# Perceiver layer on one core: the last key's context product in one piece of 128 columns for four heads

## What is computed

```python
q = (query @ Wq).reshape(b, sq, NUM_HEADS, HEAD_DIM).transpose(0, 2, 1, 3)
k = (key @ Wk).reshape(b, sk, NUM_KV_HEADS, HEAD_DIM).transpose(0, 2, 1, 3)
v = (value @ Wv).reshape(b, sk, NUM_KV_HEADS, HEAD_DIM).transpose(0, 2, 1, 3)
...
scores = jnp.einsum('bhqd,bhkd->bhqk', q, k) * scale
probs = jax.nn.softmax(scores, axis=-1)
out = jnp.einsum('bhqk,bhkd->bhqd', probs, v)
```

## Time and profile before

| | |
|---|---|
| median of 3 runs | 1096.29 us (1095.58 to 1100.33) |
| the profiled execution | 1093.26 us |
| its span in the trace | 1091.7 us |
| mean granted clock of TensorE | 0.985 |
| PE busy | 1051.1 us (96%) |
| DVE, ACT, POOL busy | 632.9, 477.7, 245.2 us |
| share of PE in the chain that ended last | 29%, the second half of the program |

### The profile page before, as it was taken

The page is one execution under the profiler, slowest core; times in us unless marked ns, Lnnn a source line. Parts: engine busy times, 40 slices in busy tenths (PEclk is TensorE's granted clock), DMA queues, the critical chain, the costliest instruction groups (busy, mean ns, idle before and its releaser), DMA issues. The chain is left out here.

```text
span 1091.7 us, 25345 instructions
## 1 busy us (share of the span) xinstructions
PE 1051.1 (96%) x9020; PEld 964.5 (88%) x9021; DVE 632.9 (58%) x1626; ACT 477.7 (44%) x1127; POOL 245.2 (22%) x414
## 2 busy tenths in 40 slices
PE   9999989999999999999999999499998799999996
PEld 9999889999999999999999999377776688888885
DVE  6641256666667666666667666648777635245220
ACT  4321245555555555554555554513323345355331
POOL 2000211211212121212112121024545333232232
PEclk9999999999999999999999999699999999999999
DMA  9442566575757565675657555464537588588432
GB/s 341 136 154 79 185 185 183 173 204 163 207 149 210 169 184 171 181 199 172 198 154 212 162 154 134 162 216 117 98 78 262 123 267 234 172 268 237 137 75 37
DMA packets 78602, 189.45 MB, mean 174 GB/s; under 512 B 16512, under 2 KB 27136, under 8 KB 74400
## 3 DMA queue, kind: packets, MB, share of 16 engines
q1 hardware_dynamic: 64096, 154.15, 45.4%
q0 software_dynamic: 14400, 33.88, 13.1%
HBM read 148.66 MB, written 44.56 MB: 177 GB/s over the span
## 5 line engine op out<-in xcount | busy, mean ns | idle before, releaser
L451 ACT ACTIVATE prob<-bank,nmax 128x257 f32<-128x257 f32 x256 | 122.0, 477 | 244.6 <-DVE nmax L590 244.4
L590 DVE TENSOR_REDUCE nmax<-bank 128x1 f32<-128x257 f32 x256 | 108.8, 425 | 160.2 <-PE bank L790 160.2
L670 PE MATMUL bank<-cT_h,wkv_h 128*128 128x256 f32 x512 | 155.0, 303 | 0.0
L679 PE MATMUL bank<-wkv_h,cT_h 128*128 128x256 f32 x512 | 154.4, 302 | 0.0
L670 PE MATMUL bank<-cT_h,wkv_l 128*128 128x256 f32 x512 | 145.0, 283 | 0.0
L670 PE MATMUL bank<-cT_l,wkv_h 128*128 128x256 f32 x512 | 144.7, 283 | 0.0
L679 PE MATMUL bank<-wkv_h,cT_l 128*128 128x256 f32 x512 | 144.5, 282 | 0.0
L679 PE MATMUL bank<-wkv_l,cT_h 128*128 128x256 f32 x512 | 143.9, 281 | 0.0
L345 POOL DMA_DIRECT2D qcat<-q_scratch x128 | 70.2, 555 | 271.6 <-PE bank L790 268.6
L705 PE MATMUL bank<-ident,prob 128*128 128x128 f32 x512 | 101.4, 280 | 10.0 <-DVE pT L245 6.8
L1640 PE MATMUL bank<-w_h,rows_h 128*128 x272 | 107.4, 395 | 0.0
(11 more groups left out here) (210 smaller groups left out, 2395.9 us busy)
## 6 DMA issues: line engine op xcount, KB each, us to landing
kcat<-k_scratch SPq DMA_DIRECT2D x128, 258.0 KB, 4.1
cx<-in_context SPq DMA_DIRECT2D x32, 1024.0 KB, 7.4
raw<-in_expert_w SPq DMA_DIRECT2D x48, 512.0 KB, 7.6
qcat<-q_scratch POOLq DMA_DIRECT2D x128, 128.0 KB, 3.2
k_scratch<-kT_h SPq DMA_DIRECT2D x32, 258.0 KB, 2.6
k_scratch<-kT_l SPq DMA_DIRECT2D x32, 258.0 KB, 3.0
x_in<-in_x SPq DMA_DIRECT2D x16, 512.0 KB, 6.2
expert_raw<-in_expert_w SPq DMA_DIRECT2D x16, 512.0 KB, 8.9
```

What stands on the lines that cost most here:

```text
L451: act.activation(prob[:, 1 - par, s, 0:SK], s_ps[s % 2][:, 0:SK], ACT.Exp, bias=nmax[:, 1 - par, s:s + 1], accum_out=sums[:, 1 - par, s:s ...
L590: dve.reduce_max(nmax[:, 1 - par, s:s + 1], s_ps[s % 2][:, 0:SK], AXX, negate=True).then_inc(max_done, 1)
L670: o = pe.matmul(k_ps[:, j * 256:(j + 1) * 256], wkv[w][:, k, j * P:(j + 1) * P], cT[t][:, b % 2, k, :], start=(j == 0 and k == 0 and n == ...
L679: o = pe.matmul(v_ps[:, a * KV:(a + 1) * KV], cT[t][:, b % 2, k, a * P:(a + 1) * P], wkv[w][:, k, KV:2 * KV], start=(a == 0 and k == 0 and ...
```

## The change

In each j the four products of 32 columns on `plT` and `vl` become one product of 128 columns over the same 128 partitions of `vl`: the columns of heads 4j to 4j + 3 lie side by side in `vl`, and the partitions of `o_ps` in the same order, so its output is the four outputs at once. The product has the same place in the order (after the eight on `pT` and `v_sb` of its j), and the last one carries the `stop` flag and `pv_done`. Nothing else is touched.

```diff
-                    for c in range(3):
+                    for c in range(2):
                         for g in range(4):
                             i = 4 * j + g
-                            values_of = v_sb[:, a % 2, c, slot_cols(i)] if c < 2 else vl[:, a % 2, slot_cols(i)]
-                            shares = pT[:, i, c * P:(c + 1) * P] if c < 2 else plT[:, :]
-                            o = pe.matmul(o_ps[g * DH:(g + 1) * DH, j * P:(j + 1) * P], values_of, shares,
-                                          start=(j == 0 and c == 0), stop=(j == 1 and c == 2), skip_group_check=True)
+                            pe.matmul(o_ps[g * DH:(g + 1) * DH, j * P:(j + 1) * P], v_sb[:, a % 2, c, slot_cols(i)], pT[:, i, c * P:(c + 1) * P],
+                                      start=(j == 0 and c == 0), stop=False, skip_group_check=True)
+                    o = pe.matmul(o_ps[:, j * P:(j + 1) * P], vl[:, a % 2, j * P:(j + 1) * P], plT[:, :],
+                                  start=False, stop=(j == 1), skip_group_check=True)
                 o.then_inc(pv_done, 1)
```

## The result

The changed kernel takes 1109.72 us in the median of 4 runs (1105.41 to 1112.52), the kernel before 1096.41 (1095.58 to 1100.33). The ratio is 1.0112, with a 95% interval from 1.0084 to 1.0141: **1.1% slower**, 13.3 us by the medians; 1109.2 was forecast. (Beside the first four experiments one more run of the kernel before took 2101.78 us, a slow run that the ratios leave out.) The profiled execution of the changed kernel took 1111.77 us, 2 us over its median.

The account below looks back on a forecast made before the run. PE was taken to bound the kernel. Per block 0.28 + 0.10 + 0.01 = 0.39 us; 30 blocks give 11.7, the last two 1.2, so 1096.3 + 12.9 = 1109.2 us; range 1101 to 1114.5.

Parts of the forecast that it names:

- PE sets the step: Attention loop: PE is busy without a gap, so anything added to a block lengthens the total once per batch element.
- The exchange gains nothing by itself: plT,vl products in each block: four of 32 columns side by side take 0.22 us, as does one of 128.
- One pair of passages, 0.28 us: Within each block: one more change from 32-column to 128-column products and back costs PE 0.28 us.
- The exposed loads, 0.10, and the pitch, 0.01: Per block: full weight loads behind 32-column work expose 0.05 us twice; loads every 0.11 against groups every 0.109 add 0.01.
- The sum, 12.9 us: Whole kernel: 30 blocks at 0.39 us give 11.7, the last two blocks 1.2; total 12.9 us slower.
- two in the tail at 0.6: Last two blocks, mostly at the lower clock: 0.6 us each, taken between 0.39 and 0.78.
- Cheap passage: Rival: wide weights load while 32-column products still work in the block, so 0.18 to 0.30 us per block; chance 0.13.
- No passage is paid: Rival: around the block the type change fp32r to f32 costs, not width; 1096.3 us or up to 0.5 less; chance 0.09.
- Dear passage: Rival: the wide product waits for every strip and its whole load, 0.45 to 0.60 us per block; chance 0.14.
- What I said the trace would show: Block on PE: 17.97 us per step, 2.44 around the block, 0.22 before the first plT record, second record 0.2 later.
- The estimate of 53 ns per drain: Skill-based price for width changes in the block: 128 cycles at 2.4 GHz, two more per block, 3.2 us in 30 blocks.

Follow-up runs that it names:

- the first four experiments: Kernels with the 128-column products both last or both first in the block, or only the second or first half changed; ratios to the kernel before 1.0013, 0.9985, 0.9986, 1.0067.
- both products first: Changed kernel with both 128-column products moved ahead of the block's sixteen 32-column ones; step 17.600 us, ratio 0.9985 to the kernel before.
- the two kernels with one half changed: Against the kernel before, only j = 1 or only j = 0 gets the 128-column product; steps 17.647 and 17.920 us, ratios 0.9986 and 1.0067.
- The 64-column products: Changed kernel with two products of 64 columns in place of each 128-column one; step 18.020 us, ratio 1.0125 to the kernel before.
- the zero product: Kernel before plus one 128-column product of zero weights on 8 moving columns between the block's halves; step 18.043 us, ratio 1.0136.
- The second half alone: Kernel before with only j = 1 given the 128-column product, j = 0 keeping its four of 32 columns; step 17.647 us, ratio 0.9986.
- the first alone: Kernel before with only j = 0 given the 128-column product, j = 1 keeping its four of 32 columns; step 17.920 us, ratio 1.0067.
- both products last: Changed kernel with both 128-column products moved behind the block's sixteen 32-column ones; step 17.637 us, ratio 1.0013 to the kernel before.
- in fp32r: 128-column products ahead of the 32-column ones, with vl, plT and the values' half of kvl as fp32r; step 17.327 us, ratio 0.9930 to the kernel before.
- the zero products of 32 columns: Kernel before plus four 32-column products of zero weights on 8 moving columns between the block's halves; step 17.650 us, ratio 1.0019.

## Why the prediction was right, point by point

**PE sets the step.** It holds. In all ten traces PE is busy without a gap from the first block to the 29th, and in the nine changed kernels what a block costs more or less shows in the step, from -0.260 to 0.456 us.

**The exchange gains nothing by itself.** Right, and shown by the order with both products first: 0.013 us per step, 0.01 of which was in the sum as the loads' pitch. Four strips side by side are one wide product.

**One pair of passages, 0.28 us.** Right: 0.27 us between the two kernels with one half changed. The 64-column products (0.433 for three more passages, 0.144 each) show that it goes by changes of width, and the zero product that it doesn't go by columns moved.

**The exposed loads, 0.10, and the pitch, 0.01.** The second half alone costs 0.060, the first alone 0.333, together 0.393, which is the measured step of the full change; it adds without remainder. The term of the load is 0.04 to 0.05 per wide product where I had 0.05 (0.037 us between the two orders, 0.050 for both products last over the kernel before); over 30 blocks the difference is under a microsecond.

**The sum, 12.9 us.** The first 28 steps give 28 x 0.393 = 11.0 us. From block 29 (655.87, and 667.49 in the changed trace) to the first L1486 product it is 54.82 us before (to 710.69) and 57.42 after, 2.6 us more, of which I had 2.0: two blocks at 0.39 and two in the tail at 0.6. Together 13.6 us to the end of attention against my 12.9. The tail's is the term that was too small: 1.8 us where I had 1.2. The rows of both tails, before and then changed, say where it went:

```profile
684.70 0.55 PE L790 MATMUL bank<-kcat,qcat 128*128 128x258 f32 x1 [2.25 <-issue]
...
688.20 1.08 PE L724 MATMUL bank<-pT,v_sb 128*32 128x128 f32 x16 [0.46 <-ACT plT L463]
...
690.33 0.43 PE L724 MATMUL bank<-plT,vl 128*32 128x128 f32 x8
690.70 0.44 PE L705 MATMUL bank<-ident,prob 128*128 128x128 f32 x2
...
704.79 1.08 PE L724 MATMUL bank<-pT,v_sb 128*32 128x128 f32 x16 [0.68 <-ACT plT L463]
```

```profile
697.35 0.36 PE L790 MATMUL bank<-kcat,qcat 128*128 128x258 f32 x1 [2.48 <-issue]
...
700.66 1.08 PE L722 MATMUL bank<-pT,v_sb 128*32 128x128 f32 x16 [0.46 <-ACT plT L463]
...
704.00 0.63 PE L705 MATMUL bank<-ident,prob 128*128 128x128 f32 x2
...
718.28 1.08 PE L722 MATMUL bank<-pT,v_sb 128*32 128x128 f32 x16 [0.67 <-ACT plT L463]
...
724.91 0.52 PE L1486 MATMUL bank<-wo_h,rows_h 128*128 128x512 f32 x1 [3.09 <-DVE rows_l L1260]
```

Blocks 29 and 30 stand ahead of these rows, at full clock, and cost 0.80 us more together, as in the loop. Then PE waits ahead of a product of line 790, 0.23 us longer than before (2.48 against 2.25). Block 31 takes 3.34 us from its start to the transposes (700.66 to 704.00), against 2.50 before, 0.84 more. But part of that is the clock: before, it came back to full within this block (eight plT records take 0.66 us at 689.05, and 0.43 at 690.33), and in the changed trace it did not. Block 32 is the clean one: its products ran at a granted clock of 0.50 to 0.53 in both traces, and from its start to L1486 are 5.90 us before and 6.63 after, 0.73 more. So at the lower clock the change costs nearly twice its 0.39, close to the upper of the two values between which I had put it. Of the 0.6 us that I lacked, 0.13 are in block 32, 0.24 in block 31 with its clock, and 0.23 in the wait.

That wait does not follow what the steps do. It is 2.25 us before, 2.48 with the change, 2.08 with both products last, 1.15 with both first, and 0.64 us or less in the other six traces. The code waits there for the loads of `kcat` and `qcat`; the trace names no releaser, and why it differs stays open. Without it the stretch from block 29 to L1486 goes by the widths: 52.6 us before, 52.6 to 53.2 in the four kernels whose step is up to 0.063 us longer, 54.5 to 55.1 in the four where it is 0.333 to 0.456 longer, and 52.0 in fp32r.

**The rest of the program.** In the profiled executions the part from the first L1486 product to the end took 381.0 us before and 385.3 after. Nothing in it was changed; the granted clock of that stretch is 0.99 before and 0.97 in the changed trace. In the ten traces it takes 381.0 to 387.2 us, 386.2 with the zero products of 32 columns and 381.2 with only the second half changed, so it does not follow the order of the products. The profiled execution of the change was 2 us over its median, that of before 3 us under it, which is these 4 us. The medians' 13.3 us agree with the 13.6 up to the end of attention.

**The rivals.** *Cheap passage* falls: 0.20 us without a load stand ahead of each wide load, and the 0.393 us lie above its 0.30. *No passage is paid* falls by the change alone, since everything in the block is f32; that the type costs nothing is seen at 215.16 to 215.28 and 215.46 to 215.73 in the orders with the wide products first. *Dear passage* falls: 0.393 us lie under its 0.45, and the step of 17.980 under the 18.03 that I had named as its sign. What I said the trace would show (17.97 per step, 2.44 us round the block, 0.22 us ahead of the wide product's first record and 0.4 behind it) came within 0.02 us (17.980, 2.44, 0.22 and 0.42).

The drain that the Trainium skill states for a change of tiling mode (TensorEngine Tiling (Array Packing), "Key Properties") agrees with these traces for 32, 64 and 128 columns: time is lost at each change of width and not between strips. The traces show the lost time and the missing loads, not the drain itself. The estimate of 53 ns per drain, made from the Trainium skill's page TensorE: Matmul & The Clock Gate ("Step-by-step: what each phase is for"), is less than half of what a passage costs here, 0.27 us for a pair.

## What to carry to other kernels

Four products of 32 columns in four column strips run in the time of one of 128, so merging them gains no PE time, and it costs one if it puts another width into the sequence: here 0.14 us for each change of width, which is more than half of the 0.22 us of the product, and up to 0.05 us for each full load of weights that follows narrower work. Count the changes of width in program order, not the products, and put the odd one beside work of its own width; then a merged product is free, and only then do its fewer records pay, in fp32r for instance. Where one engine is busy without a gap, measure the length of a loop step in the trace: it resolves 0.01 us where the totals of the same kernel spread by 5 to 9.

## What was not expected of the hardware

Few columns of weights alone did not cost a passage at one place. In the kernel before, the transposes of the last key have 8 columns and stand between transposes of 128:

```profile
213.79 0.39 PE L705 MATMUL bank<-ident,prob 128*128 128x128 f32 x2
214.01 0.27 PE L707 MATMUL bank<-ident,prob 128*8 128x128 f32 x1
214.12 0.60 PE L662 MATMUL bank<-ident,cx 128*128 128x128 f32 x4
```

The middle one (line 707) starts and is followed at the ordinary pitch of 0.11 us. Whether that is because it is a transpose, or because its output isn't placed in a strip of its own, no run here tells. The second is the fp32r record ahead of the strips. If the way in costs what it does elsewhere, it took about 0.06 us instead of 0.11. For fp32r products of 128 moving columns the load of the next weights would then set the pitch, and a product at the edge of the strips would escape it; no run here tests that by itself.
